# Three routed expert stages of a decoder: every expert's weights in a place of its own, loaded before the routing; blocks' experts read as packed words on TensorE

## The reference: what is computed

```
x = x + linear_attention(norm(x));  x = x + state_space(ctx, norm(x));  x = x + experts16_top6(norm(x))
x = x + softmax_attention(norm(x)); x = x + state_space(ctx, norm(x));  x = x + mx_feed_forward(norm(x))
x = x + feature_attention(norm(x)); x = x + context_mixing(norm(x));    x = x + experts8_top2_and_shared(norm(x))
x = x + gated_recurrence(norm(x));  x = x + cross_attention(norm(x));   x = x + experts64_top4(norm(x))
```

```
scores = softmax(h @ router.T)             # E columns
weight, chosen = top_k(scores, K)          # per token; normalised to sum 1 in the 2nd and 3rd stage
out[t] = sum over chosen e of weight * ( (silu(h[t] @ gate[e]) * (h[t] @ up[e])) @ down[e] )
```

| stage | prefix | experts E | K per token | inner width F | shared experts |
|---|---|---|---|---|---|
| third | `l0f_` | 16 | 6 | 176 | none |
| ninth | `l2f_` | 8 | 2 | 176 | 4 parts of one shared expert of width 704 |
| twelfth | `l3f_` | 64 | 4 | 192/2 = 96 | none |

## Time and profile before

### The profile page before, as it was taken

The page is one execution under the profiler, slowest core; times in us unless marked ns, Lnnn a source line. Parts: engine busy times, 40 slices in busy tenths (PEclk is TensorE's granted clock), DMA queues, the critical chain, the costliest instruction groups (busy, mean ns, idle before and its releaser), DMA issues. The chain is left out here.

```text
span 1943.4 us, 22726 instructions
## 1 busy us (share of the span) xinstructions
PE 1126.4 (58%) x5644; PEld 710.2 (37%) x5644; DVE 1129.1 (58%) x1878; ACT 473.7 (24%) x881; POOL 591.0 (30%) x616
## 2 busy tenths in 40 slices
PE   5316548994073962551696703698566278648750
PEld 2202125772042730111454502576433034437530
DVE  5759974442462637998875694411457358464324
ACT  2143302220021533320211101332122146403210
POOL 0026613445610103661100072034402022115454
PEclk9669967996586975996898856899878579969985
DMA  6024329983209002421000011244300620088762
GB/s 209 1 90 146 113 77 283 320 285 93 65 9 185 5 27 85 151 87 65 1 0 1 1 13 30 88 134 144 93 5 0 149 49 3 3 279 255 227 192 85
DMA packets 146199, 196.56 MB, mean 101 GB/s; under 512 B 35056, under 2 KB 109954, under 8 KB 145484
## 3 DMA queue, kind: packets, MB, share of 16 engines
q1 hardware_dynamic: 109996, 144.47, 25.3%
q0 software_dynamic: 12608, 31.26, 5.7%
q10 hardware_dynamic: 23520, 19.93, 3.3%
HBM read 153.55 MB, written 41.75 MB: 100 GB/s over the span
## 5 line engine op out<-in xcount | busy, mean ns | idle before, releaser
L163 PE MATMUL psum<-w_ident,h 128*128 128x128 f32 x144 | 32.5, 419 | 156.5 <-DVE h L144 156.5
L1530 DVE TENSOR_REDUCE l3x_neg<-psum 128x2 f32<-128x512 f32 x128 | 80.8, 683 | 59.6 <-PE psum L1402 59.6
L453 PE MATMUL psum<-l0s_conv_out,w_ident 128*128 128x512 f32 x128 | 65.0, 632 | 83.5 <-DVE l0s_conv_out L550 83.5
L453 PE MATMUL psum<-l1s_conv_out,w_ident 128*128 128x512 f32 x128 | 65.4, 636 | 80.0 <-DVE l1s_conv_out L550 80.0
L1505 ACT ACTIVATE l3x_work<-psum 128x512 f32<-128x512 f32 x128 | 72.5, 599 | 75.2 <-PE psum L1424 74.9
L175 ACT ACTIVATE hT<-psum 128x512 f32<-128x512 f32 x40 | 21.7, 595 | 281.2 <-PE psum L163 239.4
L152 POOL TENSOR_SCALAR rstd<-moments 128x8 f32<-128x8 f32 x12 | 2.9, 240 | 281.3 <-DVE moments L140 281.3
L163 PEld LDWEIGHTS psum<-w_ident,h 128*128 128x128 f32 x144 | 29.0, 222 | 160.2 <-DVE h L144 148.0
L419 POOL TENSOR_TENSOR l0s_xpad<-l0s_du,l0s_bc 128x1024 f32<-128x1024 f32 x32 | 75.3, 2354 | 32.5 <-DVE psum L546 32.3
L419 POOL TENSOR_TENSOR l1s_xpad<-l1s_du,l1s_bc 128x1024 f32<-128x1024 f32 x32 | 75.2, 2353 | 32.5 <-DVE psum L546 32.4
L973 PE MATMUL psum<-l0f_w_in,l0f_xT 128*128 (+1 forms) x224 | 78.5, 474 | 11.3 <-issue 11.1
(11 more groups left out here) (641 smaller groups left out, 3218.9 us busy)
## 6 DMA issues: line engine op xcount, KB each, us to landing
l0f_w_in<-in_l0f_w_in SPq DMA_DIRECT2D x56, 352.0 KB
l0s_bc<-l0s_scratch SPq DMA_DIRECT2D x16, 1024.0 KB, 5.1
l1s_bc<-l1s_scratch SPq DMA_DIRECT2D x16, 1024.0 KB, 5.2
l3f_w_in<-in_l3f_w_in SPq DMA_DIRECT2D x64, 192.0 KB
l0f_w_down<-in_l0f_w_down SPq DMA_DIRECT2D x56, 176.0 KB
l2f_w_in<-in_l2f_w_in SPq DMA_DIRECT2D x24, 352.0 KB
l3f_y_rows<-h SPq DMA_DIRECT2D x16, 512.0 KB, 6.8
l3f_y_rows<-l3f_y ACTq DMA_DIRECT2D x64, 128.0 KB
```

The costliest lines, as they stand in the source:

```text
L163: ins = nc.tensor.transpose(m.psum[:, at:at + P], m.h[:, t, k * P:(k + 1) * P], m.ident[:])
L453: ins = nc.tensor.matmul(m.pair(2 + c)[:, cols], lhsT=m.ident[:], rhs=rhs[:, cols], start=start, stop=stop, skip_group_check=True)
L1530: ins = nc.vector.tensor_reduce(self.neg[k % 2][:, :, hl], bank[:, 0:self.keys].rearrange("p (q k) -> p q k", q=self.maxima), AX_X, ALU.ma ...
```

## The change

- **Weights.** `w_in` and `w_down` now have one place for each expert (and each shared part). SP loads all E of them in order at the start of the stage, without knowing the routing. It keeps four experts in flight, and raises one semaphore, `there`, for each expert that has arrived. SP has nothing to do in the stage afterwards. The store of `h_rows` moves to ACT's queue.
- **Blocks' experts.** Instead of a row with one int per block, PE multiplies `owner` with a constant `packing`, which gives one word of 4 x 6 bits per group: two rows of words, shifted by one block and by three, for the two uses of the weights. `owners_diag` and its DVE instruction are gone. PE reads two words per group of blocks (`experts_of`), cuts each expert's number out with a shift and a mask, waits until `there` is past this expert before `w_in` is used, and addresses the weights by the expert. The two waits per block on `in_loaded` and `down_loaded` are gone from PE.
- **Unmade rows.** One `y_rows` of 24 groups serves all three stages. It is filled once, with 24 DMAs of 512 KB from `ctxT`, which SP issues in the first stage behind the weights' DMAs. The fills in the expert stages are gone.
- **Room.** `l2f_` and `l3f_` have 16 buffers for gathering back instead of 24, and all three stages use `m.h` and `m.hT` first. Most tables of the routing now share memory with `m.hT` or with the blocks' tiles. `carry` and `ctxT` are a weight group of their own, `spans`, given back after the tenth stage.

```diff
+            m.wait_weights(sp, "spans")
+            for rows in m.y_rows.rearrange("(g b p) d -> g p b d", b=GROUP, p=P):
+                sp.dma_start(rows, m.ctxT[:].rearrange("p (b d) -> p b d", d=D)).then_inc(m.y_filled, 16)
...
-BACKS = 3 * TILES
+BACKS_OF = {"l0f_": 3 * TILES, "l2f_": 2 * TILES, "l3f_": 2 * TILES}
+EXPERTS_PER_WORD = 64
...
-    w_in = sb(tag + "w_in", [P, ahead, KD, 2 * F])
-    w_down = sb(tag + "w_down", [rows, ahead, chunks, D])
-    place = lambda b: b & (ahead - 1)
+    w_in = sb(tag + "w_in", [P, routed + shared, KD, 2 * F])
+    w_down = sb(tag + "w_down", [rows, routed + shared, chunks, D])
...
-    back = [b[:] for b in ring("back", [P, D], TILES)] + [b[:, t, :] for b in (m.h, hT_rows) for t in range(TILES)]
+    BACKS = BACKS_OF[tag]
+    back = [b[:, t, :] for b in (m.h, hT_rows) for t in range(TILES)] + [
+        b[:] for b in ring("back", [P, D], BACKS - 2 * TILES)]
...
         def _(sp):
+            def load(e, k):
+                sp.dma_start(w_in[:, e, :, :].rearrange("p c x -> p (c x)"), source("w_in", e)).then_inc(in_loaded[k], 16)
+                sp.dma_start(w_down[:, e, :, :].rearrange("p c x -> p (c x)"), source("w_down", e)).then_inc(down_loaded[k], 16)
+
+            def arrived(e):
+                done = e // GROUP * 16 + 16 + EARLIER
+                sp.wait_ge(in_loaded[e % GROUP], done)
+                sp.wait_ge(down_loaded[e % GROUP], done)
+                sp.sem_inc(there, 1)
+
             for e in range(shared):
-                at = shared_place(e)
...
+                load(routed + e, e)
+            for e in range(E):
+                if e >= GROUP:
+                    arrived(e - GROUP)
+                elif shared:
+                    sp.wait_ge(in_loaded[e], EARLIER)
+                    sp.wait_ge(down_loaded[e], EARLIER)
+                load(e, e % GROUP)
+            for e in range(E - GROUP, E):
+                arrived(e)
-            sp.wait_ge(m.h_ready, TILES * (n + 1))
-            sp.dma_start(h_rows.rearrange("(t p) d -> p t d", p=P), m.h[:]).then_inc(h_stored, 16)
-
-            with sp.Fori(FEWEST, GROUPS) as i:
-                sp.dma_start(y_groups[bass.ds(i, 1)].rearrange("o b p d -> p (o b) d"),
-                             m.h[:, 0:GROUP, :]).then_inc(filled, 16)
-            groups = group_count(sp)
-            def step(base, s, first, last):
-                e = sp.value_load(owners[0:1, bass.ds(base + s, 1)], min_val=0, max_val=E - 1)
...
-            with sp.Fori(ahead // GROUP, groups) as i:
-                for s in range(GROUP):
-                    step(i * GROUP, s, False, False)
...
-                nc.tensor.matmul(owner_row, lhsT=m.w["ones"][:], rhs=owners_diag[:], start=True,
+                nc.tensor.matmul(owner_words, lhsT=owner[:], rhs=m.w["packing"][:, :, 0:GROUPS + 1], start=True,
                                  stop=True).then_inc(owners_filled, 1)
...
+            def experts_of(i):
+                found = []
+                for k in range(2):
+                    word = pe.value_load(words[0:1, k, bass.ds(i, 1)], min_val=0, max_val=(E - 1) * EVERY_EXPERT)
+                    found.append([(word >> 6 * s) & (E - 1) for s in range(GROUP)])
+                return found
...
+                    e = owners[0][s]
+                    pe.wait_ge(there, e + 1)
+                    pe.sem_inc(there_for, 1)
                     pe.wait_ge(xT_ready, base + (d + 1))
-                    pe.wait_ge(in_loaded[d % GROUP], turn(1))
...
-                        ins = nc.tensor.matmul(in_ps[d % 2], lhsT=xT[d % 2][:, k, :], rhs=w_in[:, bass.ds(place(base + d), 1), k, :].rearrange("p o x -> p (o x)"),
+                        ins = nc.tensor.matmul(in_ps[d % 2], lhsT=xT[d % 2][:, k, :], rhs=w_in[:, bass.ds(e, 1), k, :].rearrange("p o x -> p (o x)"),
...
-            by_steps(pe, groups, step, 3)
+            owners = experts_of(0)
+            for s in range(GROUP):
+                step(0, s, True, False, owners)
+            with pe.Fori(1, groups) as i:
+                owners = experts_of(i)
+                for s in range(GROUP):
+                    step(i * GROUP, s, False, False, owners)
+            owners = experts_of(groups)
+            for s in range(3):
+                step(groups * GROUP, s, False, True, owners)
         def _(act):
             norm_scalar(m, act, j)
+            act.wait_ge(m.h_ready, TILES * (n + 1))
+            act.dma_start(h_rows.rearrange("(t p) d -> p t d", p=P), m.h[:]).then_inc(h_stored, 16)
...
-            act.wait_ge(filled, (GROUPS - FEWEST) * 16)
+            act.wait_ge(m.y_filled, 16 * MOST_GROUPS)
```

More of the change, by code:

```diff
@@ L290, in _ @@
             m.wait_weights(pe, "consts")
+            m.wait_weights(pe, "spans")
             norm_tensor(m, pe, n)
@@ L595 @@
 GROUP = 4
-BACKS = 3 * TILES
+MOST_GROUPS = 24
+BACKS_OF = {"l0f_": 3 * TILES, "l2f_": 2 * TILES, "l3f_": 2 * TILES}
+EXPERTS_PER_WORD = 64
+EVERY_EXPERT = sum(EXPERTS_PER_WORD ** k for k in range(GROUP))
 def by_steps(eng, groups, step, lag):
@@ L610, in by_steps, with experts @@
         step(groups * GROUP, s, False, True)
-def experts(m, n, j, tag, routed, top, rows, chunks, ahead, shared=0, normalize=False, floor=None):
+def experts(m, n, j, tag, routed, top, rows, chunks, shared=0, normalize=False, floor=None):
     nc = m.nc
@@ L2297, in decoder @@
         loaded_x = m.sem("loaded_x")
+        m.y_filled = m.sem("y_filled")
+        m.y_rows = nc.dram_tensor("y_rows", (MOST_GROUPS * GROUP * P, D), F32).ap()
         m.gather_sems = {tag: ([m.sem(tag + f"x_loaded{i}") for i in range(GROUP)],
-                               [m.sem(tag + f"back_loaded{i}") for i in range(min(BACKS, top * TILES))])
-                         for tag, top in (("l0f_", 6), ("l2f_", 2), ("l3f_", 4))}
+                               [m.sem(tag + f"back_loaded{i}") for i in range(backs)])
+                         for tag, backs in BACKS_OF.items()}
         m.neg_sems = {tag: [m.sem(tag + f"neg_loaded{i}") for i in range(2)] for tag in ("l1a_", "l3x_")}
@@ L2318, in decoder @@
             lambda n, j: state_space(m, 0, n),
-            lambda n, j: experts(m, n, j, "l0f_", routed=16, top=6, rows=88, chunks=2, ahead=16),
+            lambda n, j: experts(m, n, j, "l0f_", routed=16, top=6, rows=88, chunks=2),
             lambda n, j: softmax_attention(m, n, j, "l1a_", heads=16, causal=True),
@@ L2324, in decoder @@
             lambda n, j: context_mixing(m, n, j),
-            lambda n, j: experts(m, n, j, "l2f_", routed=8, top=2, rows=88, chunks=2, ahead=16, shared=4, normalize=True),
+            lambda n, j: experts(m, n, j, "l2f_", routed=8, top=2, rows=88, chunks=2, shared=4, normalize=True),
             lambda n, j: gated_recurrence(m, n, j),
             lambda n, j: softmax_attention(m, n, j, "l3x_", heads=32, causal=False),
-            lambda n, j: experts(m, n, j, "l3f_", routed=64, top=4, rows=96, chunks=1, ahead=32, normalize=True, floor=1e-12),
+            lambda n, j: experts(m, n, j, "l3f_", routed=64, top=4, rows=96, chunks=1, normalize=True, floor=1e-12),
         ]
@@ L2378, in constants @@
     c["ones"] = np.ones((P, P), np.float32)
+    c["packing"] = np.zeros((P, 2, P // GROUP + 1), np.float32)
+    for i, ahead in enumerate((1, 3)):
+        for b in range(P):
+            word, digit = divmod(b + ahead, GROUP)
+            if word <= P // GROUP:
+                c["packing"][b, i, word] = EXPERTS_PER_WORD ** digit
     f = np.arange(P)
```

136 lines of the change are left out of this document (61 added, 75 removed).

## The result

The changed kernel takes 1983.93 us (median of 6 runs, 1974.19 to 1988.72) against 1961.26 for the kernel before (6 runs): ratio 1.0154, 95% interval 1.0114 to 1.0194. It is slower by 1.5%. I had forecast 1950 and a range up to 1980. (Medians are over all executions; a ratio leaves out those that are over 1.5% above the fastest of their kernel, and where the two differ I go by the ratio.) The profiled execution has a span of 1972.4 us, 29 us more than that of before.

The account below looks back on a forecast made before the run. PE was taken to bound the `l0f_` and `l2f_` loops, SP's DMA issue the late part of `l3f_`. Terms -17.5 + 5.7 - 2.4 - 3.0 + 2.1 = -15.1 us gave 1950 from 1965.1, range 1928 to 1980.

Parts of the forecast that it names:

- SP's pace goes: `l3f_` loop: weights no longer late, SP's 2.41 us a block gone, 112.8 us against 130.3, -17.5 us including PE's reads.
- my lower bound of -24: `l3f_` loop: the term's best case, reads hidden and each group at POOL's 6.74 us.
- PE's reads of words: `l3f_`: two reads cost 1.28 us a group, unhidden 5.68 + 1.28 + 0.2 = 7.16 us; inside the -17.5.
- r: Time of a group's two word reads on PE, taken as 1.28 us.
- The reads where PE bounds the loop: Nineteen groups of `l0f_` and `l2f_`: PE's queue lead nearly covers the reads, 0.3 us each, +5.7 us (bounds 0 and 28).
- Start of `l0f_`: First gather to PE's first turn falls from 6.1 us to 3.7, weights being in before routing ends: -2.4 us.
- The end of `l3f_`: The last L973's 7.80 us idle wait for weights shrinks: -3.0 us; fewer gather buffers there cost +2.1 us.
- The 16 buffers: End of `l3f_`: the seventeenth gather waits for the first addition, last gather 1931.4 instead of 1929.30, +2.1 us (upper +7.7).
- At nothing: Costed at zero: 24 fills in stage one, fills leaving expert stages, `h_rows` on ACT, dropping `owners_diag`, `l2f_`'s already early loads.
- The rival of costly reads: Expert loops: reads cost more than they free, -15.1 + 34.75 x (r - 1.28), slower, 1982 at r = 2.2; chance 0.15.
- The pauses change: Stage ends of `l0f_` and `l3f_`: unexplained pauses (14.31 and 7.80 us) shrink, 1935, to 1925 if all goes; chance 0.13.
- its sum of +5: Whole kernel: with the skill's 600 ns load, a group's reads are 1.86 us and the sum about +5, 20 us higher.

Follow-up runs that it names:

- kind 1: Batches of runs, inferred to differ by chip (9, 8 and 7 recorded), in which the kernel before has a median of 1957 to 1961 us.
- before_fourth: The kernel before, unchanged, run once more on kind 1 for its trace: one run, 1941.0 us.
- no_reads_aligned: no_reads with tiles placed as in the kernel before (outputs not the reference's): ratio 0.9840 to the kernel before, on kind 1.
- kind 2: Batches of runs, inferred to differ by chip (11 and 2), in which the kernel before has a median of 1905 to 1908 us.
- before_again: The kernel before, unchanged, run once more on kind 1: one run, 1949.2 us.
- no_reads: The changed kernel without PE's word reads, expert taken from the block's own number (outputs not the reference's): ratio 0.9915 to the kernel before, on kind 1.
- late_reads: The changed kernel with each of the two reads moved to just before its first use: ratio 1.0020 to the kernel before, on kind 1.
- read_ahead: The changed kernel, tiles placed as before, one unchecked load fetching both next-group words in the third step, behind w_in products: ratio 0.9837 to before, kind 1.
- one_read: The changed kernel with both words read by one load, without bounds check, just before first use: ratio 1.0054 to the kernel before, on kind 2.
- after_third: The changed kernel, unchanged, timed on kind 2: ratio 1.0272 to the kernel before, median 1956.5 us.
- after_aligned: The changed kernel with `packing` widened from 264 to 512 bytes per partition, restoring later tiles' offsets: ratio 1.0164 to the kernel before, median 1932.7 us, kind 2.
- before_one_y: The kernel before with its three y_rows replaced by one of 96 blocks, declared first: ratio 0.9979 to the kernel before, on kind 2.

## Why the prediction was wrong

Point by point, on the profiled executions.

- **SP's pace goes: right** on kind 1, and worth more than I took: with no reads 27 us of the loop (137.9 us between first and last turn in before_fourth, 111.1 in no_reads_aligned), 3 us beyond my lower bound of -24. On kind 2 the kernel before runs at 7.6, and there it would be 8 us (an estimate). The weights' DMAs were issued in 75 us (1714.0 to 1789.4), where I had 106.
- **PE's reads of words: the step that failed, by its overlap first and its size second.** I took r = 1.28 for two reads and let all but 0.42 of it (7.16 against 6.74) vanish under POOL's pace, because PE seemed to need only 5.68. Nothing vanished. By groups four to fifteen the loop needs 6.71 without reads and 8.14 with them at full clock: +1.43. So 6.74 was about the right pace, but not POOL's own, and rows that I had said so: both gathers of the earlier trace rows had idled until PE's L964, and the earlier trace rows had 1.79 us a block, 7.14 a group, where I took the shortest distance of two blocks, 1.42. The size was short as well, 1.46 in the queue against 1.28. And I had no term for the clock, which costs another 0.72 a group. Over 15.75 groups that is 16 us from the overlap and size and 11 from the clock (estimates from these rows). The loop took 136.9 us by the gathers of x, where I had forecast 112.8 and the earlier trace rows had 130.3: the term was -17.5 and came out at +6.6 (+4.1 by the turns of x, 8.65 to 8.91).
- **The reads where PE bounds the loop: mis-sized.** +5.7 forecast; 0.61 a group in `l0f_` and 0.78 in `l2f_`, 13.75 x 0.61 + 4.75 x 0.78 = +12.1. A lead of 1.4 us did not hide two reads in a row with what PE does with the words: apart, they cost 0.14 in `l0f_`. Two reads put into the kernel before cost 0.2 there, so the reads alone are not all of the 0.61.
- **Start of `l0f_`: right**, -2.4 forecast, first turn 42.2 us into the stage before and 38.5 after: -3.7. From the first gather to it are 3.0 us, forecast 3.7.
- **The end of `l3f_`: half wrong.** The -3.0 did not come; the stop before the last w_in product was 20.0 and is 18.6 us, with weights lying ready, so they were not its cause. The 16 buffers cost 3.0 us (last gather 21.2 us behind the first addition, give 18.2); +2.1 forecast.
- **At nothing: one thing was missing.** Stage one took 85.2 us against 84.0, and 85.3 in before_again: the fills cost nothing. But I had no line for what a new constant moves. Its cost is 23 to 24 us on chip 2, of kind 2. On kind 1 it was not measured on one chip: it is what is left of +23 for the whole after +14 for the expert stages, 9 us, or, by the ratios of no_reads and no_reads_aligned, 15 us with an uncertainty of about 13 (both estimates).

The rival of costly reads had the mechanism, but its formula at r = 1.83 gives only +4. The total needed both, the expert stages at +14 us where I had -15, and the shift that no rival had. "The pauses change" happened in `l3f_` alone and on kind 1: the stop goes from 20.0 to 12.6 in late_reads, 10.0 in read_ahead and 2.5 where the reads are gone. The same stop at the end of `l0f_` stays on kind 1 even without reads: 20.5 us before, 29.5 in the changed kernel, 25.9 in no_reads. On kind 2 both are 3 to 5 us in every kernel. What it is stays open.

The Trainium skill's 600 ns for a `tensor_load` (DMA: Bandwidth & Descriptors, "Latency and other measured facts") is not what the load takes here, 0.31. With the 0.33 of a check added, as the prediction did, it gives 0.93 for a read where the trace has 0.80 from one load to the next, and I had 0.64; its sum of +5 lay nearer to the result than mine.

## What to carry to other kernels

A register read on the engine that feeds the array costs the whole way to its next useful instruction, not the load's own duration; measure that way. Before you let such a cost vanish under another engine's pace, look at what ended that engine's waits: if it was yours, nothing vanishes. Two reads in a row also brought stretches at half clock, and setting the reads apart took these away. One load for both words, without a check, took another 0.83 us a group off the last stage; put behind queued work, it was hidden in the loop whose queue had a lead and not in that one. When an edit adds or resizes a tile, look where every later tile comes to stand: on one chip a constant of 264 bytes made 23 to 24 of the 51 us that were lost. And compare stage by stage, the untouched stages too.

## What the runs showed of the hardware

- A load of one word from SBUF into a register takes PE 0.31 us, of two 0.53 (changed, one_read). The Trainium skill (Runtime: NRT & Kernel Launch, "Instruction fetch mechanics") has some 200 ns a register for loads from HBM; the 0.22 more for the second word here agrees.
- With the array idle for 1.4 us once a group (changed), seven of twelve groups hold a stretch at 1.2 GHz and take 9.37 us instead of 8.14. With gaps of 0.87 and 0.34 instead (late_reads) none of the twelve does.
- With every tile behind the routing constants moved to 32 bytes over a multiple of 64, the program takes 23 to 24 us more on one chip; it has DMAs that pack in 512-byte pieces, whose stage was the longer one (256.0 against 221.8 us in after_third and after_aligned). The Trainium skill (DMA: Bandwidth & Descriptors, "How a descriptor splits into AXI transactions") has descriptors cut at multiples of 256 bytes. By it offsets of 64 and 128 should cost as well; the 1536-byte packets do, 77 ns against 72, but the time does not show it.
- The same program runs at 1957 or at 1907 us, as it seems by the chip. 43 of the 50 us are in two stages (before: 265.5 and 248.7 on one kind, before_one_y: 250.1 and 221.0 on the other), at the stop after the loops and in the pace of `l3f_`. Here is the stop in DVE's timeline of the kernel before. The product that it copies was done by 1879.4:

```profile
1888.90 0.29 DVE L1146 COPY l3f_gatedT<-psum 96x128 f32<-96x128 f32 x1 [11.71 <-DMA l3x_q_packed<-l3x_parts]
```

The releaser named there is a DMA of the stage before, long done: for the last 9 us the profile shows nothing that DVE waited for.
